# Four heads of 96 in three tiles, and an attention's two products in plain float32

## The reference

```python
def first_attention(latents, context):        # 16 query heads, 4 key heads, 96 wide
    hidden = concatenate([context, latents])   # 64 + 256 keys in each of 4 batches
    q = (latents @ Wq.T)                       # 512 -> 16 * 96
    k, v = hidden @ Wk.T, hidden @ Wv.T        # 512 -> 4 * 96
    attn = softmax(q @ k.T / sqrt(96))         # four query heads share a key head
    return (attn @ v) @ Wo.T                   # 16 * 96 -> 512

def last_attention(x, context):                # 32 query heads, 8 key heads, 16 wide
    q = rmsnorm(x) @ wq.T                      # 512 -> 32 * 16
    k, v = context @ wk.T, context @ wv.T      # 64 keys in each batch
    attn = softmax(q @ k.T / sqrt(16))
    return (attn @ v) @ wo.T
```

## Time and profile before

| | us |
|---|---|
| median of three runs (1760.4 to 1763.0) | 1762.4 |
| profiled execution | 1756.3 |
| its span, first to last instruction | 1754.6 |
| busy in the span: PE | 1447.6 |
| busy: DVE | 1126.1 |
| busy: ACT | 460.9 |
| busy: POOL | 312.5 |
| first attention, about | 40 to 633 |
| last attention's units | 1370 to 1541 |

### The profile page before, as it was taken

One profiled execution on the slowest core, in us unless ns is written; L12 is line 12 of the kernel. 1 busy time (PEld: TensorE's weight loads), 2 busy tenths in 40 slices (PEclk: granted clock), 3 DMA queues, 4 the chain that ended last, 5 costly groups with the idle time before them and its releaser, 6 DMA issues.

```text
span 1754.6 us, 19242 instructions
## 1 busy us (share of the span) xinstructions
PE 1447.6 (83%) x6585; PEld 1148.8 (65%) x6585; DVE 1126.1 (64%) x2623; ACT 460.9 (26%) x994; POOL 312.5 (18%) x186
## 2 busy tenths in 40 slices
PE   6559999998999889898376878589997576589998
PEld 5337777775766668686265667377875465477786
DVE  4567777767767658767966656734466788854142
ACT  3223433433333323232212113113212322222010
POOL 4101211221112112111121013115422322012120
PEclk9889999999999989899655897569998778799999
DMA  5421331322223221331011012001111000001011
GB/s 187 152 70 51 89 87 49 97 72 72 69 66 84 65 61 42 84 82 41 24 43 38 25 49 90 17 1 36 52 46 48 24 1 1 0 24 61 13 38 48
DMA packets 99410, 96.43 MB, mean 55 GB/s; under 512 B 13138, under 2 KB 72418, under 8 KB 99314
## 3 DMA queue, kind: packets, MB, share of 16 engines
q1 hardware_dynamic: 98802, 94.35, 18.3%
q0 software_dynamic: 512, 0.85, 0.2%
HBM read 84.34 MB, written 10.82 MB: 54 GB/s over the span
## 4 chain that ended last, share of the span: by engine, by line
PE 62%; DVE 26%; issue 4%; ACT 4%; DMA 2%; SPq 1%; POOL 1%; DVEq 0%; ACTq 0%; POOLq 0%
PE bank L1651 48%; PE bank L1991 5%; PE bank L1743 4%; DVE nf_y L1595 3%; DVE st L1136 2%; DVE xn L1154 2%; PE bank L1676 1%; DMA nf_a<-in_L_w 1%; DVE mx L1504 1%; DVE e L1518 1%; PE bank L1733 1%; DVE sm L1516 1%; DVE xT L1113 1%; DVE mx L1187 1%; PE bank L1947 1%
## 5 line engine op out<-in xcount | busy, mean ns | idle before, releaser
L1651 PE MATMUL bank<-xT,slots 128*128 128x512 f32 (+1 forms) x1920 | 462.7, 399 | 9.7 <-DVE xT L1113 6.3
L808 POOL TENSOR_TENSOR slots<-staging,slots 128x1024 fp32r<-128x1024 f32 (+4 forms) x97 | 230.3, 2377 | 1112.3 <-ACT slots L896 1112.2
L1651 PEld LDWEIGHTS bank<-xT,slots 128*128 128x128 f32 (+1 forms) x1920 | 351.9, 184 | 107.7 <-issue 9.4
L1595 DVE TENSOR_SCALAR nf_y<-nf_w 128x512 fp32r<-128x512 f32 (+2 forms) x495 | 233.8, 499 | 25.3 <-PE bank L1991 24.3
L1651 PE MATMUL bank<-slots,h 128*128 128x512 f32 (+1 forms) x728 | 181.6, 410 | 20.1 <-DVE h L1243 13.9
L1651 PEld LDWEIGHTS bank<-slots,h 128*128 128x128 f32 (+1 forms) x728 | 142.9, 197 | 56.8 <-DVE h L1243 14.8
L1991 PE MATMUL bank<-nf_y,nf_d 128*128 128x512 f32 (+2 forms) x495 | 168.8, 425 | 11.3 <-DVE nf_y L1595 9.0
L896 ACT ACTIVATE slots<-staging 128x1024 fp32r<-128x1024 f32 (+4 forms) x97 | 98.1, 1018 | 187.8 <-PE bank L1651 173.7
L929 ACT ACTIVATE e<-bank,mx 128x320 f32<-128x320 f32 x128 | 66.3, 523 | 274.3 <-DVE mx L1190 270.3
L1209 DVE TENSOR_TENSOR x<-bank,x 128x512 f32<-128x512 f32 x72 | 49.7, 691 | 125.0 <-PE bank L1651 125.0
L1991 PEld LDWEIGHTS bank<-nf_y,nf_d 128*128 128x128 f32 (+1 forms) x495 | 94.2, 195 | 47.6 <-DVE nf_y L1595 16.9
(11 more groups left out here) (244 smaller groups left out, 1942.7 us busy)
## 6 DMA issues: line engine op xcount, KB each, us to landing
staging<-in_L_wqkT SPq DMA_DIRECT2D x16, 480.0 KB, 3.6
nf_out<-nf_w SPq DMA_DIRECT2D x30, 256.0 KB, 2.1
staging<-nf_out SPq DMA_DIRECT2D x30, 256.0 KB, 2.8
staging<-in_L_woT SPq DMA_DIRECT2D x16, 384.0 KB, 3.5
staging<-in_L_w SPq DMA_DIRECT2D x12, 512.0 KB, 4.0
nf_a<-nf_max SPq DMA_DIRECT2D x40, 128.0 KB, 3.6
nf_r<-nf_rcp SPq DMA_DIRECT2D x40, 128.0 KB, 3.5
nf_w<-in_L_w SPq DMA_DIRECT2D x15, 256.0 KB, 4.1
```

Of the source, the lines that this page charges most:

```text
L808: g.tensor_tensor(lo, split_source(i), hi.bitcast(FP32), ALU.subtract).then_inc(*sig.mark("weight_low", i))
L1595: v.tensor_scalar(nf_y[0:rows, i % STAIR_RING, 0:size], w_, bound, first, compare, ALU.mult)\
L1651: ins = mm(dst, l_, r_, start=i == 0, stop=i == len(passes) - 1)
```

## The change

For the first attention, the 384 rows of four query heads are laid out in three tiles of 128: tile j holds head j in rows 0 to 95 and rows 32 j to 32 j + 31 of the fourth head in rows 96 to 127 (`spare(j)`). The weights are reordered on the host for it. The query step exists three times in a stage; ACT copies rows 0 to 95 to head j's place and rows 96 to 127 to the fourth head's place, partitions 32 j and up, and DVE does the same for the low part. The value product of the fourth head is written back in three pieces of 32 rows into rows 96 to 127 of the three tiles. The output product sums three tiles of 128 rows. The second chunk of output weights holds one tile instead of two.

For the last attention, queries, keys, values and turned probabilities are kept once in float32, copied by ACT alone; the scores and the value products are plain float32 matmuls. The low parts of all of these go (their DVE handlers `k3_`, `v3_`, `q3_`, `turn3` too), POOL masks one key tile per unit instead of two, DVE places two copies instead of four. The result of the value product is still split, into a buffer of its own (`a3`).

The diff, without bookkeeping of names and signals:

```diff
@@ -94,6 +95,11 @@
+def spare(j):
+    return slice(j * SPARE0, (j + 1) * SPARE0)
@@ -107,7 +113,7 @@
-    steps += [("k0", 0), ("kc0", 0)] + [("q0", 0, h) for h in range(HPG)]
+    steps += [("k0", 0), ("kc0", 0)] + [("q0", 0, j) for j in range(QT0)]
@@ -132,7 +138,7 @@
-                steps += [("q0", s + 1, h) for h in ((0, 1), (2,), (3,))[j - 5]]
+                steps.append(("q0", s + 1, j - 5))
@@ -377,7 +383,7 @@
-        q0 = sb("q0", [HD0, 2, 2, HPG, HALF], F32R, s0)
+        q0 = sb("q0", [P, 2, 2, HPG, HALF], F32R, s0)
@@ -442,13 +448,14 @@
-        q3 = sb("q3", [P, 2, KT, TOK], F32R, l)
-        kd3 = sb("kd3", [P, 2, 2, HPC, CTX], F32R, l)
-        vd3 = sb("vd3", [P, 2, 2, PAIRS, P], F32R, l)
-        kr3 = sb("kr3", [P, 2, KT, B * CTX], F32R, l)
-        v3 = sb("v3", [CTX, 2, B, KV3 * HD3], F32R, l)
+        q3 = sb("q3", [P, KT, TOK], FP32, l)
+        kd3 = sb("kd3", [P, 2, HPC, CTX], FP32, l)
+        vd3 = sb("vd3", [P, 2, PAIRS, P], FP32, l)
+        kr3 = sb("kr3", [P, KT, B * CTX], FP32, l)
+        v3 = sb("v3", [CTX, B, KV3 * HD3], FP32, l)
...
-        eT3 = sb("eT3", [P, 2, PAIRS, S], F32R, l)
+        eT3 = sb("eT3", [P, PAIRS, S], FP32, l)
+        a3 = sb("a3", [P, 2, 2, KT, S], F32R, l)
@@ -491,9 +498,9 @@
         def o0_chunks(s):
-            for i in range(2):
-                rows = a["L0_woT"][(s % G0 * HPG + 2 * i) * HD0:(s % G0 * HPG + 2 * i + 2) * HD0]
-                chunk(("o0", s, i), HD0, (2, D), [((slice(None),), rows.rearrange("(h p) n -> p h n", p=HD0))])
+            for i, n in enumerate((2, 1)):
+                rows = a["L0_woT"][(s % G0 * QT0 + 2 * i) * P:(s % G0 * QT0 + 2 * i + n) * P]
+                chunk(("o0", s, i), P, (n, D), [((slice(None),), rows.rearrange("(h p) n -> p h n", p=P))])
@@ -819,14 +826,11 @@
-                pool.wait_ge(*sig.when("k3_low", c))
+                pool.wait_ge(*sig.when("k3_kept", c))
...
-                for part in range(2):
-                    ins = g.tensor_tensor(kd3[:, n % 2, part],
-                                          kr3[:, part, c, b * CTX:(b + 1) * CTX].bitcast(FP32).unsqueeze(1).broadcast_to((P, HPC, CTX)),
-                                          hm3[:].unsqueeze(2).broadcast_to((P, HPC, CTX)), ALU.mult)
-                ins.then_inc(*sig.mark("keys3", n))
+                g.tensor_tensor(kd3[:, n % 2], kr3[:, c, b * CTX:(b + 1) * CTX].unsqueeze(1).broadcast_to((P, HPC, CTX)),
+                                hm3[:].unsqueeze(2).broadcast_to((P, HPC, CTX)), ALU.mult).then_inc(*sig.mark("keys3", n))
@@ -918,8 +927,11 @@
             def kc0_(s):
...
-            def q0_(s, h):
-                high("q0", (s, h), q0[:, s % 2, 0, h], psum(("q0", s, h))[0:HD0])
+            def q0_(s, j):
+                bank = psum(("q0", s, j))
+                act.wait_ge(*sig.when("q0_product", (s, j)))
+                sc.activation(q0[0:HD0, s % 2, 0, j], bank[0:HD0], ACT.Copy)
+                sc.activation(q0[spare(j), s % 2, 0, QT0], bank[HD0:P], ACT.Copy).then_inc(*sig.mark("q0_high", (s, j)))
@@ -941,7 +953,14 @@
             def pv0(n, s, bl, h):
-                high("pv0", n, q0[:, s % 2, 0, h, bl * S:(bl + 1) * S], psum(("pv0", n))[0:HD0, 0:S])
@@ -1058,14 +1077,12 @@
             def turn3(n, b, c):
...
-                    act.wait_ge(*sig.when("turn3_product", (n, i)))
...
-                    sc.activation(eT3[:, 0, 2 * i:2 * i + 2], psum(("turn3", n, i))[:].rearrange("p (k n) -> p k n", k=2),
-                                  ACT.Copy).then_inc(*sig.mark("turn3_high", (n, i)))
+                    keep("turn3", (n, i), eT3[:, 2 * i:2 * i + 2], psum(("turn3", n, i))[:].rearrange("p (k n) -> p k n", k=2))
...
             def pv3(n, b, c):
-                high("pv3", n, q3[:, 0, c, b * S:(b + 1) * S], psum(("pv3", n))[:, 0:S])
+                high("pv3", n, a3[:, b % 2, 0, c], psum(("pv3", n))[:, 0:S])
@@ -1178,8 +1195,11 @@
-            def q0_(s, h):
-                low("q0", (s, h), q0[:, s % 2, 1, h], psum(("q0", s, h))[0:HD0], q0[:, s % 2, 0, h])
+            def q0_(s, j):
+                bank = psum(("q0", s, j))
+                dve.wait_ge(*sig.when("q0_high", (s, j)))
+                v.tensor_tensor(q0[0:HD0, s % 2, 1, j], bank[0:HD0], q0[0:HD0, s % 2, 0, j].bitcast(FP32), ALU.subtract)
+                low("q0", (s, j), q0[spare(j), s % 2, 1, QT0], bank[HD0:P], q0[spare(j), s % 2, 0, QT0])
@@ -1198,8 +1218,15 @@
             def pv0(n, s, bl, h):
-                cs = slice(bl * S, (bl + 1) * S)
-                low("pv0", n, q0[:, s % 2, 1, h, cs], psum(("pv0", n))[0:HD0, 0:S], q0[:, s % 2, 0, h, cs])
+                cs, bank = slice(bl * S, (bl + 1) * S), psum(("pv0", n))
+                if h < QT0:
+                    low("pv0", n, q0[0:HD0, s % 2, 1, h, cs], bank[0:HD0, 0:S], q0[0:HD0, s % 2, 0, h, cs])
+                    return
+                dve.wait_ge(*sig.when("pv0_high", n))
+                for j in range(QT0):
+                    ins = v.tensor_tensor(q0[HD0:P, s % 2, 1, j, cs], bank[spare(j), 0:S],
+                                          q0[HD0:P, s % 2, 0, j, cs].bitcast(FP32), ALU.subtract)
+                ins.then_inc(*sig.mark("pv0_low", n))
@@ -1470,31 +1497,20 @@
             def values3(n, b, c):
...
-                dve.wait_ge(*sig.when("v3_low", b))
+                dve.wait_ge(*sig.when("v3_kept", b))
...
-                for part in range(2):
-                    src = v3[:, part, b, c * groups * HD3:(c + 1) * groups * HD3].bitcast(FP32)\
-                        .rearrange("p (u d) -> p u d", d=HD3).unsqueeze(2).broadcast_to((CTX, groups, PAIRS // groups, HD3))
-                    for j in range(2):
...
-                        blocks = vd3[CTX * j:CTX * (j + 1), n % 2, part].rearrange("p q (a d) -> p (q a) d", d=HD3)
-                        dst = blocks[:, j::HPC + 2].rearrange("p (u w) d -> p u w d", u=groups)
-                        ins = v.tensor_copy(dst, src)
+                src = v3[:, b, c * groups * HD3:(c + 1) * groups * HD3]\
+                    .rearrange("p (u d) -> p u d", d=HD3).unsqueeze(2).broadcast_to((CTX, groups, PAIRS // groups, HD3))
+                for j in range(2):
...
+                    blocks = vd3[CTX * j:CTX * (j + 1), n % 2].rearrange("p q (a d) -> p (q a) d", d=HD3)
+                    dst = blocks[:, j::HPC + 2].rearrange("p (u w) d -> p u w d", u=groups)
+                    ins = v.tensor_copy(dst, src)
@@ -1518,16 +1534,8 @@
-            def turn3(n, b, c):
-                for i in range(2):
-                    dve.wait_ge(*sig.when("turn3_high", (n, i)))
-                    v.tensor_tensor(eT3[:, 1, 2 * i:2 * i + 2], psum(("turn3", n, i))[:].rearrange("p (k n) -> p k n", k=2),
-                                    eT3[:, 0, 2 * i:2 * i + 2].bitcast(FP32), ALU.subtract)\
-                        .then_inc(*sig.mark("turn3_low", (n, i)))
...
             def pv3(n, b, c):
-                cs = slice(b * S, (b + 1) * S)
-                low("pv3", n, q3[:, 1, c, cs], psum(("pv3", n))[:, 0:S], q3[:, 0, c, cs])
+                low("pv3", n, a3[:, b % 2, 1, c], psum(("pv3", n))[:, 0:S], a3[:, b % 2, 0, c])
@@ -1709,18 +1716,18 @@
-            def q0_(s, h):
+            def q0_(s, j):
...
-                bank = claim(("q0", s, h), ("q0_low", (s, h)))
-                qk(s, ("q0_product", (s, h)), h * HD0, (h + 1) * HD0, lambda k: xt(k, hf * HALF, (hf + 1) * HALF), bank[0:HD0])
+                bank = claim(("q0", s, j), ("q0_low", (s, j)))
+                qk(s, ("q0_product", (s, j)), j * P, (j + 1) * P, lambda k: xt(k, hf * HALF, (hf + 1) * HALF), bank[:])
...
             def scores0(n, s, bl, h):
-                pe.wait_ge(*sig.when("q0_low", (s, h)))
+                pe.wait_ge(*sig.when("q0_low", (s, min(h, QT0 - 1))))
...
-                    l_ = [q0[:, s % 2, p, h, bl * S + i * P:bl * S + (i + 1) * P] for p in range(2)]
+                    l_ = [q0[0:HD0, s % 2, p, h, bl * S + i * P:bl * S + (i + 1) * P] for p in range(2)]
@@ -1749,8 +1756,8 @@
-                pairs = [([q0[:, s % 2, p, h, i * P:(i + 1) * P] for p in range(2)], [w[h // 2][p][:, h % 2] for p in range(2)])
-                         for h in range(HPG)]
+                pairs = [([q0[:, s % 2, p, j, i * P:(i + 1) * P] for p in range(2)], [w[j // 2][p][:, j % 2] for p in range(2)])
+                         for j in range(QT0)]
@@ -1923,24 +1930,23 @@
-                bank = claim(("q3", c, hf), ("q3_low", (c, hf)))
+                bank = claim(("q3", c, hf), ("q3_kept", (c, hf)))
...
             def scores3(n, b, c):
-                pe.wait_ge(*sig.when("q3_low", (c, b // BPH)))
+                pe.wait_ge(*sig.when("q3_kept", (c, b // BPH)))
...
-                    product(bank[:], [([q3[:, q, c, t * P:(t + 1) * P] for q in range(2)],
-                                       [kd3[:, n % 2, q].rearrange("p h k -> p (h k)") for q in range(2)])])\
```

(20 more changed lines are left out.)

38 lines of the change are left out of this document (21 added, 17 removed).

## The result

The changed kernel is slower. It took 1786.59 us (median of 4 runs, 1781.36 to 1792.52) against 1762.46 for the kernel before in the same batch: a ratio of 1.0134, 95% interval 1.0107 to 1.0162. The forecast was 1732. The profiled execution took 1786.6 us, its span 1784.9. The profiled execution of the kernel before was 6 us faster than its median, so the two spans lie 30.3 us apart and the medians 24.1.

A forecast was written before the change was run, and what follows sets the result against it. PE was taken to bound the first attention, DVE mostly the last. First attention -27, behind it +2, last attention -5: -30 us, giving 1732 for the median (1726 profiled), range 1708 to 1750.

The forecast's parts named there:

- the pieces: First attention: extra ACT copies and DVE subtractions for the spread fourth head, mostly hidden by idle time; +12 us, between 0 and +24.4.
- the planner: Background steps: some 8 move out of the first attention, -2 us there and +2 us behind it.
- the share of the cut that arrives: First attention: 0.85 of the 41.9 us of removed matmuls shortens the chain, -35.6 us, ends -31.8 and -41.9.
- TensorE's 41.9 us of matmuls: First attention: 192 query and output matmuls removed, 44.6 us, or 41.9 without the first stage's query product.
- the factor 0.85: First attention: share of removed matmul time taken to lie on the chain, chosen between 0.76 and 1.
- The slower rival: First attention: DVE's in-order remainder of the spread head sets the pace, PE's cut becomes idle time; +31 us, 1793, chance 0.05.
- POOL's shorter subtraction: First attention: the halved second chunk of output weights shortens POOL's subtraction from 2.37 to about 1.2 us, less DVE stall; -1 us.
- The last attention: Last attention: plain float32 scores and value products, with fewer DVE and POOL operations; sum -5 us, ends -13 and +5.
- this term: Last attention, nine units without an output product behind them: cycles of 7.7 to 9.6 us by clock, -6 to +8, taken as 0.

The follow-up runs named there:

- the cut alone: Three query tiles, fourth head handled in one piece, its queries left zero, old plan, against the kernel with only the last attention changed (1756.5 us): 1736.82 us.
- the square: Four kernels, old plan, last attention changed: four query tiles with one piece 1756.5, three pieces 1774.9; three tiles with one piece 1736.8, three pieces 1768.2 us.
- the pieces alone: As many extra 32-row copies and subtractions as the change adds, put into the kernel with only the last attention changed (1756.5 us): 1774.93 us.
- The packing with the plan kept: The whole change, with the planner counting the first query step twice so background steps stand as in the kernel before: 1768.17 us, ratio 1.0035.

## Why the prediction was wrong, point by point

The forecast lay 54.6 us too low. By the runs, three of its terms made nearly all of that: the pieces, which idle time was to hide (some 19 us), the planner, put at nothing net (18), and the share of the cut that arrives (16).

- **TensorE's 41.9 us of matmuls: right in number, wrong in worth.** The group counts 279 output records in the stretch, and nine matmuls take 2.10 us. But the cut was worth 6.8 to 28.8 us by what stood beside it, 20 where nothing was spread, and never 35.6. The step that failed is the factor 0.85: it was chosen between 0.76, made from TensorE's share of the chain *before* the cut, and 1. A share read before a cut says nothing of who leads once part of it is gone. One part can be named: the granted clock of the stretch went from 0.98 to 0.96 in the kernel with the cut alone, which on 448 busy us is about 9 us by my estimate. Where the other 7 us or so went isn't shown; TensorE's waits for the background compares (`nf_y`) were 10.0 us in that stretch against 0.3 in the kernel before.
- **The pieces: priced by their length, +12; measured +18.5 without the cut and +31.4 beside it.** The lengths held (0.421, 0.69). What failed is the sentence that 109 us of idle VectorE would hide them. The number itself is in no row: the stretch has 490 - 353 = 137 idle us. And this idle time was not spare: 65 us of it stood in the earlier trace rows, ahead of the remainders (50.5 and 14.4), with ScalarE as the releaser. A piece adds on ScalarE, then on VectorE, in series: 2 x (0.37 + 0.42) = 1.6 us a unit where I had counted 0.84. Over 16 units that is 25 us. The queries' 16 further pieces, each 0.59 on ScalarE and 0.69 on VectorE, are another 21. Of these 46 us 18.5 arrived without the cut, and 31.4 of 56 (24 query pieces) beside it. That they stand in a round trip is shown by two edits that leave the work as it is: a signal for each copy gave 14.5 us back, and all subtractions behind the maxima 13.1 more. The spread head's subtractions alone behind the maxima gave nothing, so it is the round trip of all units and not that of the spread ones.
- **The slower rival had the mechanism** (VectorE waits for three copies, then subtracts three times before the next maxima) and got a chance of 0.05, because "The idle DVE of the earlier trace rows speaks against it." It was the same idle time, read wrongly twice. The rival's 1793 is near the result by luck of its terms: it had the cut at nothing, the pieces at +24.4, the plan at +2 and the last attention at +5, and the runs have -20, +31, +18 and -6.
- **The planner, +2: the largest miss beside it, +18 to +25.** I had counted how many steps move (some 8; the traces have 7 fewer compares ahead of the first feed-forward, 330 against 337) and priced them as work. A part of the cost (6.3 us) is where the last one lands: ahead of or behind a serial stretch that other engines wait for. A count can't show that; writing out the order of both plans would have.
- **POOL's shorter subtraction, -1:** not separable in any run.
- **The last attention, -5: right.** It gave 4.6 in the changed kernel's trace and 6.2 alone. The parts held too where the clock stayed up. In two units of the changed kernel, at a granted clock of 1.00 from 1440 to 1452 us:

```profile
1440.43 0.69 DVE L1534 TENSOR_TENSOR e<-e,mx 128x512 f32<-128x512 f32 x1
...
1441.89 1.88 PE L1944 MATMUL bank<-kd,q 128*128 128x512 f32 x4
...
1442.95 0.69 DVE L1520 TENSOR_REDUCE mx<-bank 128x8 f32<-128x512 f32 x1 [1.20 <-PE bank L1944]
...
1448.11 0.69 DVE L1534 TENSOR_TENSOR e<-e,mx 128x512 f32<-128x512 f32 x1
```

  A cycle is 7.68 us (7.7 forecast); VectorE waits 1.20 us before the maxima, which in the earlier trace rows it did not; a score tile is 0.94 (0.91 taken, between 0.85 and 0.97). The Trainium skill (FP8 and Floating Point Precision, TensorE Precision Notes) states four passes for true FP32, which makes 0.93 us by the forecast's estimate. The trace agrees with it within a hundredth. Not every unit ran so: the nine cycles without an output product behind them took 7.7 to 9.2 us, 75.4 in all, against 8.2 to 8.8 and 76.4 before, so this term gave 1 us where 0 was taken, and 9.6 was never reached. Which way the clock would go was left open in the forecast; it rose. At the second and third unit, POOL's operations halved to 2.49 us and VectorE's copies to 2.03, as forecast.

The steps from the kernel before to the changed one, one kernel to the next: -6.2 (last attention) -19.7 (cut) +31.4 (pieces) +18.4 (plan) = +23.9. They add up by the way they are made and prove nothing by that; in another order the same parts have other sizes, as the square shows.

## What to carry to other kernels

Before idle time of an engine is taken as cover, look at what ends it: idle time that another engine's copy ends is a link of a round trip, and work added to either engine lengthens it, more so the more the bound engine is relieved. When a spread or a split adds pieces on two engines, signal each piece and put the second engine's part behind the work that the next unit waits for; here that turned 1786.6 us into 1744.4 with the same operations, while the kernel without the packing gained nothing from the new order. And when an edit changes what a planner sees, compare the two plans at every serial stretch before pricing the edit, or hold the plan still and measure the edit alone.

## What was not expected of the hardware

- The clock was lower in each of these kernels in which TensorE was idle longer, with less work as with the same, though not in the order of that idle time: granted from 150 to 640 us were 0.98 before (27 us idle), 0.96 with the cut alone (42), 0.95 with the pieces alone (30), 0.94 in the changed kernel (55). In the last attention, where plain float32 keeps TensorE busier (106 us of 153 against 103 of 158), the clock rose from 0.80 to 0.85.
- The packing with the plan kept differed more from run to run than the kernel before: 1760.8 to 1782.2 us against 1757.3 to 1767.7 in the same batch. Other packed kernels did not (1748.7 to 1758.8 with the spread head's subtractions behind), so no cause is claimed.
